# Choosing experts beside the logits, normalising on ScalarE, and an inversion with its operands exchanged, in a two-layer transformer kernel on one Trainium2 core

## The reference

```
layer 0:  logits = n @ Wg + bg + bias           (16 experts)
          vals, idx = top_k(logits, 2);  w = softmax(vals)
layer 1:  n = layernorm(x) * g1 + be1
          p = softmax(n @ Wg + bg)              (8 experts)
          vals, idx = top_k(p, 2);       w = vals / sum(vals)
both:     out = sum over the two of  w_k * (act(n @ W1[idx_k] + b1[idx_k]) @ W2[idx_k] + b2[idx_k])
```

## Time and profile before

| | |
|---|---|
| median of 3 runs | 2486.95 us (2485.18 to 2489.42) |
| the profiled execution's own time | 2488.63 us |
| its span, first to last instruction | 2486.8 us |
| mean granted clock of TensorE | 0.889 |
| busy: PE, PEld | 2028.1 us (82%), 955.6 us (38%) |
| busy: DVE, ACT, POOL | 1989.5 us (80%), 1537.1 us (62%), 562.4 us (23%) |
| layer 0: logits, route, inversion | 344.99 to 437.12 us |
| layer 1: logits, route, inversion | 2131.81 to 2231.04 us |

### The profile page before, as it was taken

One profiled execution on the slowest core, in us unless ns is written; L12 is line 12 of the kernel. 1 busy time (PEld: TensorE's weight loads), 2 busy tenths in 40 slices (PEclk: granted clock), 3 DMA queues, 4 the chain that ended last, 5 costly groups with the idle time before them and its releaser, 6 DMA issues. The chain is left out here.

```text
span 2486.8 us, 45503 instructions
## 1 busy us (share of the span) xinstructions
PE 2028.1 (82%) x16896; PEld 955.6 (38%) x16896; DVE 1989.5 (80%) x3274; ACT 1537.1 (62%) x3022; POOL 562.4 (23%) x686
## 2 busy tenths in 40 slices
PE   6999775882689999999998769999999999459920
PEld 5888564661312222222222312222222222349920
DVE  7888557666879999999993779999999995476636
ACT  5554330342329989989897519988989889106510
POOL 2444300767410000000000320000000000306455
PEclk9999975895759999999999769999999999559965
DMA  5000010344521111011100441010110100302212
GB/s 195 1 1 1 1 42 1 85 89 128 160 58 33 33 30 34 24 38 28 34 6 15 137 124 33 19 43 21 32 42 21 41 7 10 124 4 74 68 53 58
DMA packets 94412, 121.16 MB, mean 49 GB/s; under 512 B 23665, under 2 KB 56561, under 8 KB 93937
## 3 DMA queue, kind: packets, MB, share of 16 engines
q1 hardware_dynamic: 73712, 78.92, 11.4%
q0 software_dynamic: 8960, 18.37, 3.3%
q10 hardware_dynamic: 11520, 20.98, 2.7%
HBM read 69.70 MB, written 42.99 MB: 45 GB/s over the span
## 5 line engine op out<-in xcount | busy, mean ns | idle before, releaser
L1549 DVE TENSOR_REDUCE mx<-psum 128x1 f32<-128x1024 f32 x1024 | 1174.7, 1214 | 76.8 <-PE psum L1437 75.8
L1526 ACT ACTIVATE p<-psum 128x512 f32<-128x512 f32 x2048 | 1102.4, 596 | 108.5 <-PE psum L1459 66.6
L1471 PE MATMUL psum<-p,v_ext 128*32 128x256 f32 x8192 | 656.3, 392 | 39.3 <-ACT p L1526 39.2
L1437 PE MATMUL psum<-ks,qs 64*128 64x512 bf16 x2048 | 635.9, 395 | 53.3 <-DVE mx L1549 29.7
L1459 PE MATMUL psum<-qs,ks 64*128 64x512 bf16 x2048 | 630.4, 383 | 1.5 <-ACT p L1526 1.3
L1471 PEld LDWEIGHTS psum<-p,v_ext 128*32 128x32 f32 x8192 | 162.0, 108 | 473.9 <-ACT p L1526 254.3
L1459 PEld LDWEIGHTS psum<-qs,ks 64*128 64x128 bf16 x2048 | 123.8, 93 | 404.1 <-ACT p L1526 367.8
L1339 POOL CAST m_near<-mx 128x16 bf16<-128x16 f32 x128 | 25.3, 197 | 1079.6 <-DVE mx L1549 1075.5
L759 ACT ACTIVATE hid<-psum,stage 128x128 f32<-128x128 f32 x448 | 132.5, 367 | 178.0 <-PE psum L729 178.0
L703 POOL DMA_INDIRECT x_in<-n_rows,token_of x152 | 153.7, 1011 | 296.8 <-POOLq L85 219.6
L1437 PEld LDWEIGHTS psum<-ks,qs 64*128 64x128 bf16 x2048 | 118.9, 94 | 115.5 <-DVE mx L1549 81.0
(11 more groups left out here) (244 smaller groups left out, 2145.1 us busy)
## 6 DMA issues: line engine op xcount, KB each, us to landing
qs<-qk_parts SPq DMA_DIRECT2D x128, 104.0 KB
ks<-qk_parts SPq DMA_DIRECT2D x128, 104.0 KB
qk_parts<-piece__1 ACTq DMA_DIRECT2D x40, 256.0 KB, 3.8
qk_parts<-piece__2 ACTq DMA_DIRECT2D x40, 256.0 KB, 3.4
answers<-y_out SPq DMA_DIRECT2D x152, 64.0 KB, 1.5
ew<-in_moe SPq DMA_DIRECT2D x1, 5136.0 KB, 18.8
ew<-in_moe SPq DMA_DIRECT2D x1, 4624.0 KB, 14.1
n_rows<-n_all SPq DMA_DIRECT2D x8, 512.0 KB, 3.2
```

Source lines behind the costliest of these rows:

```text
L1437: pe.matmul(psum[:, bank, :], a["qs"][r, g % NKF, j % KM, i * P:(i + 1) * P], a["ks"][r, g % NKF, j % KM, k * HALF:(k + 1) * HALF], start= ...
L1471: last = pe.matmul(psum[GR * j:GR * j + VW, O_BANK, q], t["v_ext"][:, b * NT + i, VE * (h0 + j):VE * (h0 + j) + VW], a["p"][:, (GH * s + j ...
L1526: act.activation(a["p"][:, n % NP, :], psum[:, S_BANK + n % NS, :], ACT.Exp, scale=DH ** -0.5)\
L1549: dve.tensor_reduce(a["mx"][:, g % 2, h, j, 0, c:c + 1], psum[:, bank:bank + 2, :].rearrange("p a c -> p (a c)"), AX.X, ALU.max)\
```

## The change

Five things are changed in the mixture's first three stages.

- Choice beside the logits: `gate_logits` becomes `choose`. What `pick_two` did for 32 tiles at once, the one-hots and the two counting matmuls are now done batch by batch (`take`, `pick`, `count`) within the stage that makes the logits. The weights of the two choices move behind the slots in `route`.
- Normalising: ACT applies scale and shift to the eight tiles of a batch (`normalise`), in both layers; DVE computes only the two numbers for each row (`scale`). In layer 1 PE transposes the rows without g1 and be1, and ACT's copy of the transposes applies them as per-partition operands. POOL still applies them to the rows, now behind the transposes.
- The expert of each slot tile is found with slot tiles along the partitions (128 x 16 or 128 x 8 elements instead of one partition with 1280 or 576), and turned by PE in `invert`. `route` has 18 or 11 matmuls (`WARM_ROUTE`) whose result nobody reads.
- Inversion: `hi_hot` is stationary and `lo_hot` moves; DVE compares for a whole chunk (`hi_eq`), ACT multiplies each pair's row with the token number, and the list is turned by one transpose at the end.
- Loads: `load_experts(0)` moves from the kernel's start to the start of the first mixture, behind the load of `consts`, which gets a semaphore of its own.

```diff
-def route(nc, t, layer, E, tiles):
+def route(nc, t, w, layer, E, tiles):
...
         def _(pe):
-            pe.wait_ge(both_ready, 1)
-
-            both_flat = both[:, :, :].rearrange("p t e -> p (t e)")
-            pe.matmul(psum[:, 0, 0:TE], t["before"][:, :], both_flat, start=True, stop=True)
-            pe.matmul(psum[:, 1, 0:TE], t["ones"][:, :], both_flat, start=True, stop=True).then_inc(counted, 1)
+            for i in range(WARM_ROUTE[layer]):
+                pe.matmul(psum[:, 0, 0:HALF // 2], w.att[layer][5], t["y_t"][:, 0:HALF // 2], start=True, stop=True)
...
-            row = [1, tiles, E]
-            link(dve.tensor_tensor(t["ended"][:, 0:tiles, :], iota[0:1, 0:tiles].unsqueeze(2).to_broadcast(row),
-                                   end[0:1, 0:E].unsqueeze(1).to_broadcast(row), ALU.is_ge))
-            link(dve.tensor_reduce(t["who"][:, 0:tiles], t["ended"][:, 0:tiles, :], AX.X, ALU.add))
-            dve.tensor_scalar(t["expert_of"][:, 0:tiles], t["who"][:, 0:tiles], float(E - 1), None, ALU.min)
             dve.tensor_copy(t["slot_of"][:, :, :], sel[:, :, :])
+
+            link(dve.tensor_scalar(t["ended"][:, 0:E], end[:, 0:E], t["token"][:, 0:1], None, ALU.is_lt))
+            link(dve.tensor_reduce(t["who"][:, :], t["ended"][:, 0:E], AX.X, ALU.add))
...
 def invert(nc, t, tiles):
+        @block.scalar
+        def _(act):
+            for n in range(pairs):
+                if n % G == 0:
+                    act.wait_ge(eq_ready, n // G + 1)
+                if n >= 2 * G:
+                    act.wait_ge(used, n - 2 * G + 1)
+                act.activation(t["hi_hot"][:, n % (2 * G), 0:tiles], hi_eq[:, n // G % 2, n % G, :], ACT.Copy,
+                               scale=t["token"][:, n // 2:n // 2 + 1]).then_inc(hi_ready, 1)
...
-                for n in range(c * G, (c + 1) * G):
-                    dve.tensor_scalar(t["hi_hot"][:, n % (2 * G), 0:tiles], t["iota"][:, 0:tiles],
-                                      flat(hi)[:, n:n + 1], t["token"][:, n // 2:n // 2 + 1],
-                                      ALU.is_equal, ALU.mult).then_inc(hi_ready, 1)
-            dve.wait_ge(used, pairs)
-            link(dve.tensor_scalar(t["token_f"][:, 0:tiles], psum[:, 2, 0:tiles], -1.0, 0.0, ALU.add, ALU.max))
-            dve.tensor_copy(t["token_of"][:, 0:tiles], t["token_f"][:, 0:tiles])
+                if c >= 2:
+                    dve.wait_ge(hi_ready, G * (c - 1))
+                dve.tensor_tensor(hi_eq[:, c % 2, :, :], t["iota"][:, 0:tiles].unsqueeze(1).to_broadcast([P, G, tiles]),
+                                  flat(hi)[:, c * G:(c + 1) * G].unsqueeze(2).to_broadcast([P, G, tiles]),
+                                  ALU.is_equal).then_inc(eq_ready, 1)
+            dve.wait_ge(named, 1)
+            dve.tensor_scalar(t["expert_of"][:, 0:tiles], psum[0:1, 3, 0:tiles], float(t["E"] - 1), None, ALU.min)
+            dve.wait_ge(used, pairs)
+            dve.tensor_scalar(t["token_f"][0:tiles, :], psum[0:tiles, 2, 0:P], -1.0, 0.0, ALU.add, ALU.max).then_inc(listed, 1)
+            dve.wait_ge(list_turned, 1)
+            dve.tensor_copy(t["token_of"][:, 0:tiles], psum[:, 4, 0:tiles])
...
-                last = pe.matmul(psum[:, 2, 0:tiles], t["lo_hot"][:, (n // G) % 2, n % G, :],
-                                 t["hi_hot"][:, n % (2 * G), 0:tiles], start=(n == 0), stop=(n == pairs - 1))
+                last = pe.matmul(psum[0:tiles, 2, 0:P], t["hi_hot"][:, n % (2 * G), 0:tiles],
+                                 t["lo_hot"][:, (n // G) % 2, n % G, :], start=(n == 0), stop=(n == pairs - 1))
...
-def gate_logits(nc, t, w, layer, E, x, n):
+def choose(nc, t, w, layer, E, x, n):
...
-                    pool.wait_ge(tile_ready, NT * (b + 1))
+                    pool.wait_ge(turned, NT * (b + 1))
...
+            def normalise(b):
+                act.wait_ge(scales_ready, b + 1)
+                for i in range(NT):
+                    act.activation(n[b][:, i, :], src[b][:, i, :], ACT.Identity, scale=t["rstd"][:, b % 2, i:i + 1],
+                                   bias=t["shift"][:, b % 2, i:i + 1]).then_inc(tile_ready, 1)
...
+            for b in range(B + 1):
+                if b + 1 < B:
+                    root(b + 1)
+                if b < B:
+                    normalise(b)
+                if b:
+                    copy_turned(b - 1)
+                if layer and b >= B - 1:
+                    exponent(b - B + 1)
...
-                    if not layer:
-                        pe.wait_ge(tile_ready, NT * b + i + 1)
-                    elif i == 0:
-                        pe.wait_ge(shifted, b + 1)
+                    pe.wait_ge(tile_ready, NT * b + i + 1)
...
+            def count(b):
+                pe.wait_ge(both_ready, b + 1)
+                c, v = slice(b * NT * E, (b + 1) * NT * E), both[:, b * NT:(b + 1) * NT, :].rearrange("p t e -> p (t e)")
+                pe.matmul(psum[:, 6, c], t["before"][:, :], v, start=True, stop=True)
+                pe.matmul(psum[:, 7, c], t["ones"][:, :], v, start=True, stop=True)
...
+            dve.wait_ge(t["consts_loaded"], 16 * (layer + 1))
+            if layer:
+                take(0)
+                take(1)
+                for b in range(B):
+                    pick(b)
+                    if b + 2 < B:
+                        take(b + 2)
+            else:
+                for b in range(B):
+                    take(b)
+                    pick(b)
...
-            load_experts(0)
...
-                nc.sync.dma_start(consts[:, :], consts_in).then_inc(t["moe_loaded"], 16)
+                nc.sync.dma_start(consts[:, :], consts_in).then_inc(t["consts_loaded"], 16)
+                load_experts(layer)
```

More of the change, by code:

```diff
@@ L60 @@
 INV = 8
+WARM_ROUTE = (18, 11)
 PLACES = 8
@@ L539, in _ @@
                                       x[b][:, s, :], ALU.add).then_inc(x_summed, 1)
[L542 to L571, removed]
@@ L574, in route @@
-def route(nc, t, layer, E, tiles):
+def route(nc, t, w, layer, E, tiles):
     psum, T, TE = t["psum"], B * NT, B * NT * E
-    lg, sel, oh0, oh1, both, pos, cnt, upto = (t[k] for k in ("lg", "sel", "oh0", "oh1", "both", "pos", "cnt", "upto"))
+    sel, oh0, oh1, pos, cnt, upto = (t[k] for k in ("sel", "oh0", "oh1", "pos", "cnt", "upto"))
+    mx, wt, tmp = t["mx8"], t["wt"], t["tmp2"]
     per, end, base = t["per"], t["end"], t["base"]
     L3 = [P, T, E]
[L581 to L590, removed]
+    with stage(nc, "step", "to_exp", "exped") as (block, step, to_exp, exped):
@@ L896, in _ @@
                     logits(b - 1)
+            pe.wait_ge(t["consts_loaded"], 16 * (layer + 1))
+            for b in range(B):
+                count(b)
         @block.vector
@@ new lines, in pick @@
+            def pick(b):
+                s = slice(b * NT, (b + 1) * NT)
+                v, L3 = lg[:, s, :], [P, NT, E]
+                if layer:
+                    dve.wait_ge(exped, b + 1)
+                    link(dve.tensor_reduce(tmp2[:, s, 0], v, AX.X, ALU.add))
+                    link(dve.reciprocal(tmp2[:, s, 1], tmp2[:, s, 0]))
+                    link(dve.tensor_tensor(v, v, tmp2[:, s, 1:2].to_broadcast(L3), ALU.mult))
+                for i in range(b * NT, (b + 1) * NT):
+                    last = dve.max(mx[:, i, :], lg[:, i, :])
+                link(last)
+                for i in range(b * NT, (b + 1) * NT):
+                    last = dve.max_index(ix[:, i, :], mx[:, i, :], lg[:, i, :])
+                link(last)
+                link(dve.tensor_copy(sel[:, s, :], ix[:, s, 0:2]))
+                experts = t["iota"][:, 0:E].unsqueeze(1).to_broadcast(L3)
+                dve.tensor_tensor(oh0[:, s, :], experts, sel[:, s, 0:1].to_broadcast(L3), ALU.is_equal)
+                link(dve.tensor_tensor(oh1[:, s, :], experts, sel[:, s, 1:2].to_broadcast(L3), ALU.is_equal))
+                dve.tensor_tensor(both[:, s, :], oh0[:, s, :], oh1[:, s, :], ALU.add).then_inc(both_ready, 1)
@@ new lines, in _ @@
+            measure(0)
+            for b in range(B):
+                if b + 1 < B:
+                    measure(b + 1)
+                scale(b)
+            dve.wait_ge(t["consts_loaded"], 16 * (layer + 1))
+            if layer:
+                take(0)
+                take(1)
+                for b in range(B):
+                    pick(b)
+                    if b + 2 < B:
+                        take(b + 2)
+            else:
+                for b in range(B):
+                    take(b)
+                    pick(b)
@@ L1747, in build @@
         room_for_experts(8, 4)
-        load_experts(1)
         mixture(1, 8, 4, ACT.Gelu, 72)
```

112 lines of the change are left out of this document (68 added, 44 removed).

## The result

The changed kernel takes 2452.98 us (median of 4 runs, 2448.63 to 2454.47) against 2486.3 (4 runs, 2485.18 to 2489.42): a ratio of 0.986, 95% interval 0.9844 to 0.9875, so 33 us less. I had forecast 2443.5 and a range of 2431 to 2465.

The account below looks back on a forecast made before the run. Six short stages run one after another, the inversions bound by PE at half clock. Gains 9.8 + 1.9 + 11.9 + 0.4 + 2 x 9.6 + 0.3 = 43.5 us give 2445.1 profiled, 2443.5 as median; range 2431 to 2465.

Parts of the forecast that it names:

- Logits and choice, layer 0: Layer 0's first stage: copy of the counts starts 37.9 us after the stage's start instead of 47.7, gain 9.8 us.
- costs nothing: Layer 0's logits: the slower ScalarE normaliser adds no time, logits end at 31.4 us where they ended at 31.6.
- Route: Route stages: gain 1.9 us in layer 0 and 0.4 in layer 1, the added matmuls counted as hidden.
- signs that I had named as wrong: Wrong would be: 0.50 through the inversion, ScalarE above 0.29 us a scaling, or added matmuls ending after VectorE in route.
- Logits and choice, layer 1: Layer 1's first stage: copy of the counts at 48.2 us instead of 60.1 despite GpSimd's holds, gain 11.9 us.
- rival (2): Layer 1's choice: GpSimd's holds eat the whole gain there, kernel at 2455.4 us; chance 0.08.
- Inversion: Inversions of both layers: 21.3 us where 30.9 stood, the clock rising after a half-clock start; gain 9.6 us twice.
- the 64 pairs in 16.5 to 17.7: Inversion: all 64 pairs, counted as one uninterrupted stream, take 16.5 to 17.7 us after a first pass at 3.5.
- rival (4): Inversion: VectorE, ScalarE and PE take turns over two buffers, 7.3 us a chunk, kernel at 2527 us; chance 0.03.
- turning point: Inversion: from 5.1 us a chunk on, each inversion is 12 us longer than before and the other gains are used up.
- Rival (1): Inversions stay at half clock and the exchange moves nothing: 22 us go back, kernel at 2465.5 us; chance 0.18.
- Load and expert tiles: Expert weights' moved load: nothing gained, 17 us of cover; 0.3 us for a slightly better clock at the expert tiles' start.

Follow-up runs that it names:

- the leave-out: The changed kernel without GpSimd's multiplication by g1 and addition of be1 on layer 1's stored rows, a price only: 2485.93 us, ratio 0.9826.

## Why the prediction held, and where it was off

The direction, the places and the mechanisms were as forecast; the measured median is 9.5 us above the forecast. That divides into 3.5 us that the traces show (2448.63 against the 2445.1 forecast for the profiled execution), 4.4 us by which the changed kernel's median lies above its profiled execution, and 1.6 us that I took off because before's profiled execution lay above its median.

- **Logits and choice, layer 0.** Forecast 9.8 us, measured 11.0. The copy of the counts stands 36.7 us after the statistics, forecast 37.9; the logits end at 30.4, forecast 31.4. My sentence that the slower normaliser "costs nothing" was too modest: by the run in which VectorE normalises, it brings 2.3 us here and 5.4 in layer 1. With it undone the stage still lies 8.7 and 6.6 us below before; that this is the choice's new place is read by elimination, since no run puts the choice back by itself.
- **Route.** Forecast 1.9 and 0.4, measured 1.7 and -0.4. In layer 0 the added matmuls end 10.8 us after their start, forecast 9.8 to 11. In layer 1 they take 8.0 us, forecast 6.5 to 7.8, and end 0.8 us behind VectorE, which is one of the signs that I had named as wrong. The sum had them at nothing; without them the stretch from the copy to the inversion is 8.1 us instead of 8.7, which is most of the 0.8 by which this term missed. No run shows the new search for each slot tile's expert by itself.
- **Logits and choice, layer 1.** Forecast 11.9, measured 12.0. The third scales were held by three operations, not four, and the leave-out prices the holds at 6.3 us (bound: 7), 5.5 in the scales and 0.8 in the first pick, for which I had 1 to 2. Moving GpSimd's start moves the holds onto the first pick, where they cost 6.5. This rules rival (2) out: the holds are there and eat a third of what the stage could gain, not all.
- **Inversion.** This is the mis-sized term: "the 64 pairs in 16.5 to 17.7" us were 19.5 in layer 0 (397.2 to 416.7) and 19.0 in layer 1, and the gain was 6.8 and 7.3 us instead of 9.6 twice, 5.1 short together. The 21.3 us of the sum hold 16.6 for the pairs, the low end of my own range. The first pair came at 3.7 us (forecast 3.5), the clock rose 3.6 us later, and ScalarE took 0.26 a scaling (forecast 0.25). What failed is the assumption that two buffers are enough for the three engines to overlap: a chunk took 2.33 us at full clock, where ScalarE's work on it is 2.07. Of the 2.9 us by which layer 0's pairs exceed 16.6, the three waits of 0.5 between pairs of chunks make 1.5, and the first two chunks, partly at half clock, took 6.0 us instead of 4.66, another 1.3. Two buffers pass that loss on as well: three made the pairs one stream of 16.2 us, with the same half-clock start. In rival (4) I had named this mechanism, engines waiting for one another over two buffers, but only in its extreme form of 7.3 us a chunk; what came was 0.26 us a chunk, and it had no place in the sum. The turning point that I gave with it, 5.1 us a chunk, is also wrong: 12 us above the 30.9 are 43, and less 4.7 for start and end, over eight chunks, that is 4.8.
- **The clock.** Rival (1) is out. That the exchange is what raises it is shown from both sides: 0.50 without it, 0.88 with it alone. By the Trainium skill's rule for the load and the spacing of matmuls (TensorE: Matmul & The Clock Gate, "LDWEIGHTS" and "Back-to-back issue gap") the exchange alone would move nothing at equal clock, and the trace agrees: at half clock a pass starts every 0.213 us both ways.
- **Load and expert tiles.** The load moved for nothing, as forecast. For the 0.3 us of a better clock there, full clock in the first tiles brought no time.

Left open is the scatter. The changed kernel's executions lie 5.8 us apart on the first chip and 12.6 on another, with the clock lowest in the longer ones, and the profiled one was the shortest in both. Only that one has a trace, so where the longer ones lose their 3 to 13 us isn't known.

## What to carry to other kernels

When a chain of three engines works over a ring of buffers, lay out one whole turn of the ring: producer, middle engine, consumer and the release back to the producer; with two buffers the release came 0.5 us late every second chunk, and one more buffer (3.1 us an inversion) was worth more than keeping the clock up (1.2 to 1.4). Which operand of a narrow matmul moves can decide TensorE's clock, and then the bound passes to whoever makes the operands, so both edits belong together. An engine that holds another by a shared access holds whatever stands on the chain at that time: shift its start only if slack is waiting there.

## What the runs showed of the hardware

- 128 passes with 128 columns loaded and 80 or 72 streamed ran without a gap for over 24 us at a granted clock of 0.50, in the kernel before and again with ScalarE as the maker; with 80 or 72 loaded and 128 streamed the clock rose 2.8 to 5.5 us after the first pair in every run (3.6 and 4.1 in the changed kernel), unless matmuls ahead of it had kept it up.
- The passes themselves cost the same either way at equal clock, 0.213 us at 0.50.
- In the changed kernel the clock fell when the pairs were already running: 1.00 over 3.67 us of an almost idle PE, then 0.53 over 3.50 us of a busy one. In the other runs with the same matmuls in route and none in the gap it fell between 1.7 us ahead of the first pair and 0.7 us behind it. Eight matmuls in that gap kept it at 1.00.
- The same kernel takes 1.7 to 1.8% longer in the later runs, which I take to be on other chips, mostly in the expert tiles (165 for 147 us in layer 0) and the parts between, while the six stages of this change last the same to 0.4 us.
